# Gate stage stores transposed rows for the mixer, and the three stages run in one block

## The reference, cut to what matters

```python
xn  = layernorm(x)                              # no gain, no bias
# mixer
xin, xg = split(xn @ W_in.T)                    # 512 -> 2 x 1024
u   = silu(causal_conv4(xin) + conv_b)
Bu  = u @ W_B.T;  h_t = 0.95 h_(t-1) + 0.05 Bu_t    # 64 states, a scan over 2048 rows
y   = ((h @ W_C.T + D * u) * silu(xg)) @ W_out.T    # 1024 -> 512
a   = layernorm(y + xn) * g + b
# experts
gates = (tanh(xn @ gate_w.T) + 1) / 2           # 8 experts
idx   = top 1024 rows of each expert by its gate
o     = gelu(layernorm(xn[idx]) @ fc1.T + b1) @ fc2.T + b2      # 512 -> 2048 -> 512
out   = x + a + (xn with gates * o added at idx)
```

## Time and profile before

| what | value |
|---|---|
| median of 3 runs | 2914.63 us (2913.05 to 2925.31) |
| profiled execution, its own time | 2916.93 us |
| its span | 2915.2 us |
| mean granted TensorE clock | 0.986 |
| PE busy | 2794.6 us (96%) |
| DVE busy | 1849.0 us (63%) |
| ACT busy | 1309.0 us (45%) |
| POOL busy | 668.7 us (23%) |
| moved by DMA | 283.71 MB, mean 97 GB/s |

### The profile page before, as it was taken

One profiled execution on the slowest core, in us unless ns is written; L12 is line 12 of the kernel. 1 busy time (PEld: TensorE's weight loads), 2 busy tenths in 40 slices (PEclk: granted clock), 3 DMA queues, 4 the chain that ended last, 5 costly groups with the idle time before them and its releaser, 6 DMA issues.

```text
span 2915.2 us, 40359 instructions
## 1 busy us (share of the span) xinstructions
PE 2794.6 (96%) x12424; PEld 2234.5 (77%) x12426; DVE 1849.0 (63%) x3098; ACT 1309.0 (45%) x2197; POOL 668.7 (23%) x909
## 2 busy tenths in 40 slices
PE   7789999999999999999799999999999999999997
PEld 3367888888887778888687878888788787887886
DVE  6457777777777788888755554555545554455553
ACT  3354444443343355555344444444444444444443
POOL 2243222222222222223311221012210111102211
PEclk9899999999999999999899999999999999999999
DMA  7742333333333333336314133041330413304121
GB/s 270 255 139 92 108 111 109 111 112 115 115 115 116 116 88 108 96 105 210 106 34 119 30 94 81 18 128 30 94 80 16 123 37 87 77 26 123 38 44 15
DMA packets 130326, 283.71 MB, mean 97 GB/s; under 512 B 14640, under 2 KB 14832, under 8 KB 130032
## 3 DMA queue, kind: packets, MB, share of 16 engines
q1 hardware_dynamic: 98096, 183.71, 19.4%
q0 software_dynamic: 32064, 97.85, 13.8%
HBM read 226.68 MB, written 54.82 MB: 97 GB/s over the span
## 4 chain that ended last, share of the span: by engine, by line
PE 47%; issue 2%; DMA 1%; DVE 1%; POOL 0%; ACT 0%; DVEq 0%; POOLq 0%; SPq 0%
PE po L1661 8%; PE po L1662 8%; PE po L1663 8%; PE ph L1661 8%; PE ph L1663 7%; PE ph L1662 7%; PE f_pt L1670 1%; DMA out_dram<-res,idx_c 1%; DMA rows<-xn_rows,idx_c 0%; POOL out_dram L1530 0%; DMA b<-b_in 0%; DVE res L1643 0%; DVE f_stats L504 0%; DVE hid_l L1621 0%; DVE w2l L1587 0%
## 5 line engine op out<-in xcount | busy, mean ns | idle before, releaser
L1661 PE MATMUL po<-w2h,hid_h 128*128 128x512 f32 x1024 | 405.6, 396 | 14.3 <-DVE hid_l L1621 14.3
L1299 PE MATMUL ring<-xt_h,w_h 128*128 128x512 f32 x1024 | 402.5, 393 | 10.6 <-ACT sg L1029 9.2
L1662 PE MATMUL po<-w2l,hid_h 128*128 128x512 f32 x1024 | 403.1, 394 | 0.0
L1301 PE MATMUL ring<-xt_h,w_l 128*128 128x512 f32 x1024 | 402.0, 393 | 0.0
L1663 PE MATMUL po<-w2h,hid_l 128*128 128x512 f32 x1024 | 401.7, 392 | 0.0
L1300 PE MATMUL ring<-xt_l,w_h 128*128 128x512 f32 x1024 | 400.0, 391 | 0.0
L1621 DVE TENSOR_TENSOR hid_l<-xn_tail,hid_h 128x512 fp32r<-128x512 f32 x256 | 175.5, 685 | 331.8 <-ACT hid_h L1578 326.2
L1119 DVE SCALAR_TENSOR_TENSOR u<-xin,cw,u 128x512 f32<-128x512 f32 x384 | 295.4, 769 | 118.2 <-ACT u L1011 97.4
L1574 ACT ACTIVATE xn_tail<-ph,b1c 128x512 f32<-128x512 f32 x256 | 176.2, 688 | 357.1 <-PE ph L1663 348.9
L1530 POOL DMA_INDIRECT out_dram<-res,idx_c x64 | 109.4, 1709 | 898.8 <-DVE res L1643 884.2
L1548 ACT CAST w1h<-w1r 128x512 fp32r<-128x512 f32 x258 | 160.3, 621 | 280.1 <-PE po L1663 268.5
(11 more groups left out here) (176 smaller groups left out, 5561.9 us busy)
## 6 DMA issues: line engine op xcount, KB each, us to landing
wo<-wo_halves POOLq DMA_DIRECT2D x120, 512.0 KB, 4.1
w1r<-fc_in SPq DMA_DIRECT2D x130, 256.0 KB, 2.7
w2r<-fc_in SPq DMA_DIRECT2D x130, 256.0 KB, 2.9
xn_rows<-g_ext SPq DMA_DIRECT2D x16, 1040.0 KB, 5.3
w1r<-x_in SPq DMA_DIRECT2D x16, 1024.0 KB, 7.8
rows<-xn_rows SPq DMA_DIRECT2D x16, 1024.0 KB, 6.5
xn_tail<-xn_rows SPq DMA_DIRECT2D x64, 256.0 KB, 2.6
x_tail<-x_in SPq DMA_DIRECT2D x64, 256.0 KB, 2.9
```

Of the source, the lines that this page charges most:

```text
L1299: pe.matmul(ring[r % 2][:, :], w_h[:, r, q], xt_h[:, k, :], start=(k == 0), stop=False)
L1301: last = pe.matmul(ring[r % 2][:, :], w_l[:, r, q], xt_h[:, k, :], start=False, stop=(k == KD - 1))
L1661: pe.matmul(dst, ah, bh, start=start, stop=False)
L1662: pe.matmul(dst, ah, bl, start=False, stop=False)
```

## The change

- `xn_rows` is gone. The gate stage now stores the transposed rows, as ACT copied them out of the banks (1 MB for a block, `xt_rows`), and the gates alone (`gate_rows`, 8 numbers for a row). Normalising is in place and PE waits for all four tiles of a block.
- The mixer loads a turn's transposed rows as they are. Its 240 transposes are gone for turns 1 to 15; `xt_h` and `xt_l` are made from the loaded tile. The gate stage takes block 0 last, and makes turn 0's `xt_h` and `xt_l` from its own banks.
- The 16 tiles of the in-projection's weights are split in the gate stage, one for each block: ACT `w_high` behind the tanh, POOL `w_low` behind its work for the inverse deviation. POOL also gets four small instructions for each block that keep scale and shift of every row.
- The rows that the turns end with are made on ACT from `x`: `normal_rows` (for xn) and `sum_rows` (for x + xn, in place of POOL's `add_x`), four of each in a turn. The transfers into `xn_tail` are gone.
- The experts' rows are gathered from `x`, and the gates by a second gather (`gather_gates`), four more indirect transfers in a group; `keep` waits for them.
- One block holds all three stages, each engine goes from stage to stage by its own waits, and the semaphores are set once, by SP, behind the first two loads of `x`. Banks and tiles are laid over each other; the last block's gates are finished inside turn 0.

```diff
-        m.start()
-        with nc.Block() as block:
...
+    def turn(b, i):                       # POOL, gate stage
+            pool.tensor_scalar(std[:, :], mv[i % 2][:, :, 1], EPS, None, ALU.add).then_inc(c_eps, 1)
+            pool.wait_ge(c_eps, b + 1 + 1)
+            pool.tensor_tensor(rstd[i % 2][:, :], std[:, :], half[:, :], ALU.pow).then_inc(c_rs, 1)
+            pool.wait_ge(c_rs, b + 1 + 1)
+            pool.tensor_tensor(shift[i % 2][:, :], mv[i % 2][:, :, 0], rstd[i % 2][:, :],
+                               ALU.mult).then_inc(c_nb, 1)
...
+        def w_low(b, i):
+            tile = bass.ds(b, 1)
+            pool.wait_ge(c_wh, b + 1 + 1)
+            pool.sem_inc(p_tick, 1)
+            pool.tensor_tensor(w_l[:, tile, :].rearrange("p o d -> p (o d)"), w_raw[i][:, :],
...
+        with pool.Fori(1, NG - 1) as h:
+            for i in range(R):
+                turn(h * R + i, i)
+                w_low(h * R + i, i)
...
+        def group(h, first=False, last=False):          # ACT, gate stage
...
+                for k in range(KD):
+                    act.wait_ge(c_t, b * KD + k + 1 + 1)
+                    act.copy(xnt[i][:, k, :], pt[k][:, :]).then_inc(c_tc, 1)
+                    if last and i == R - 1:
+                        act.copy(ew.yt_h[0][:, k, :], pt[k][:, :]).then_inc(c_th, 1)
+                if not (first and i == 0):
+                    turn_tanh(act, b - 1)
+                if not (last and i == R - 1):
+                    w_high(b, h, i)
+                act.wait_ge(c_se, (b + 1) * KD + 1)
+                act.wait_ge(c_sc, b + 1)
+                act.copy(sc_t[:, :], pst).then_inc(c_sr, 1)
...
+    def normal_rows(self, act, b, j):
+        act.activation(self.xn_rows[j][:, :], self.x_rows[j][:, :], ACT.Identity, bias=self.row_shift[:, here],
+                       scale=self.row_scale[:, here]).then_inc(self.c_nr, 1)
...
+    def sum_rows(self, act, b, j):
+        act.activation(self.x_rows[j][:, :], self.x_rows[j][:, :], ACT.Identity, bias=self.row_shift[:, here],
+                       scale=self.twice[:, j:j + 1]).then_inc(self.c_s, 1)
...
             for k in range(KD):                        # ACT, end of a mixer turn
                 y_high(b, 4 + k)
                 side(4 + k)
-                if k >= lag:
-                    t_high((b + 1) * KD + k - lag, k - lag)
+                if not last:
+                    t_high(b, k)
+                elif k >= 1:
+                    group_high(k - 1)
+                ends.normal_rows(act, b, k)
...
-                        if 3 <= c < 7 and not last:
-                            next_turn(b, c - 3, False)
...
-            for j in range(J):                         # POOL, mixer turn
-                ends.add_x(pool, b - 1, j)
+            ends.twice_scale(pool, b - 1)
+            for j in range(J):
                 ends.add_beta(pool, b - 1, j)
...
+    def gather_gates(self, pool, g, j, i=0):
+        pool.wait_ge(self.c_mv, (g + 1) * J + 1)
+        pool.sem_inc(self.p_tick, 1)
+        pool.indirect_dma_start(
+            out=self.rows[:, j, D:XW], out_offset=None, in_=self.t["gate_rows"][:, :],
...
     def keep(self, dve, g, i):
+        for j in range(J):
+            dve.wait_ge(self.c_ga[j], 32 * (g + 1))
```

More of the change, by code:

```diff
@@ L45, in sb, with over @@
         return tile
[L47 to L69, removed]
+    def over(self, name, end, size, shape, dt=F32):
+        return self.nc.alloc_sbuf_tensor_at(name, shape, dt, offset=end - size)
 def f(ap):
@@ new lines, in stage_gate @@
+    tanh = m.sb("g_tanh", [P, J * E])
+    gw = m.sb("g_gw", [P, KD, E])
+    staged2 = m.over("g_staged2", ends.xn_end, J * D * 4, [P, 4, TB])
+    pt = banks[0:KD]
+    pst = banks[6][0:E, :]
+    psc = banks[7][:, 0:J * E]
+    w_raw = ends.res
+    w_h, w_l = ew.w1, ew.w2
+    c_id = m.count("g_id")
+    c_gw = m.count("g_gw_in")
+    c_x = [m.count(f"g_x_in{i}") for i in range(R)]
+    c_raw = ends.c_raw
+    c_wh = m.count("g_wh")
+    c_wl = sums.c_in_low
+    c_gd = sums.c_gate_rows
+    c_xs = sums.c_xt_store
@@ new lines, in turn_scores, with turn_tanh @@
+    def turn_scores(pe, b):
+        pe.wait_ge(c_sr, b + 1 + 1)
+        pe.wait_ge(c_ta, b + 1)
+        pe.sem_inc(t_tick, 1)
+        for j in range(J):
+            last = pe.transpose(psc[:, j * E:(j + 1) * E], sc_t[:, j * P:(j + 1) * P],
+                                ident[0:E, 0:E])
+        last.then_inc(c_sc, 1)
+    def turn_tanh(act, b):
+        act.wait_ge(c_sc, b + 1 + 1)
+        act.wait_ge(c_v, b * 2 + 1)
+        act.activation(tanh[:, :], psc, ACT.Tanh).then_inc(c_ta, 1)
@@ new lines, in stage_mixer @@
+    m = mem
+    w_h, w_l = ew.w1, ew.w2
+    xt_h, xt_l = ew.yt_h[0], ew.yt_l[0]
+    rows = ew.rows
+    w_raw = ends.res
+    ls = Lists(m, gates, thr, slots_d, ew, sums)
+    wo = m.sb("wo", [P, WO, 2, D], F32R)
+    u = m.sb("u", [P, NC_, TB])
+    u_h = [m.sb(f"u_h{i}", [P, TB], F32R) for i in range(2)]
+    u_l = [m.sb(f"u_l{i}", [P, TB], F32R) for i in range(2)]
+    y_h, y_l = u_h, u_l
+    sg = m.sb("sg", [P, SG, TB])
+    xin = [m.sb(f"xin{i}", [P, 3 + TB]) for i in range(2)]
+    halo = m.sb("halo", [P, NC_, 3])
@@ new lines, in stage_mixer @@
+    po, c_o, c_po = ends.po, ends.c_o, ends.c_po
+    p_tick, d_tick = ends.p_tick, ends.d_tick
+    c_win = ends.c_raw
+    c_wo = [m.tick(f"m_wo{s}") for s in range(WO)]
+    c_ws = m.count("m_ws")
+    c_rows = m.count("m_rows")
+    c_set = m.count("m_set")
+    c_wh = m.count("m_wh")
+    c_wl = m.count("m_wl")
+    c_ag = m.count("m_ag")
+    c_x = m.count("m_x")
+    c_hi = m.count("m_hi")
+    c_ho = sums.c_ho
+    c_ev = m.count("m_ev")
+    c_cv = sums.c_cv
+    c_u = m.count("m_u")
+    c_uh = m.count("m_uh")
@@ L873, in _ @@
-                with sp.Fori(1, LAST) as b:
-                    turn(b)
-                for dst, src in ((ew.gamma, t["f_ln_g"]), (ew.beta, t["f_ln_b"])):
-                    sp.dma_start(dst[:, :], src.to_broadcast([P, D])).then_inc(ew.c_small, 16)
-                last_turn(LAST)
+                gate[0](sp)
+                mixer[0](sp)
+                experts[0](sp)
             @block.gpsimd
             def _(pool):
-                pool.memset(ends.half[:, :], -0.5).then_inc(c_set, 1)
@@ L1709, in build @@
[L1709 to L1726 removed]
+                gate[4](act)
@@ L1729 @@
+                mixer[4](act)
+                experts[4](act)
 SHAPES = {
```

2327 lines of the change are left out of this document (1199 added, 1128 removed).

## The result

The changed kernel takes 2905.84 us, the median of 6 runs (of which one took 7964.04 us and is left out of the comparison; the others lie between 2903.56 and 2908.58), against 2916.68 us for the kernel before in 6 runs. The ratio is 0.9958, with a 95% interval of 0.9945 to 0.9972. The profiled execution has a span of 2906.9 us against 2915.2, so 8.3 us less.

What follows compares the result with a forecast made beforehand. PE is busiest; some 70 us of its idle time lie before turn 1 and at turn 15. Terms 18.8 - 20.4 + 3 - 5 - 4.8 = -8.4 against 2916.93 give 2908.5, as a median 2906 us; range 2880 to 2936.

Steps and rivals of the forecast that it cites:

- Gate stage: Gate stage: loop ACT, POOL, DVE, PE gives 9.3 us a block (8.37 to 9.77); turn 0 starts 18.8 us later.
- Turn 0: Mixer's first turn: without step-by-step weight feed 77.0 us instead of 97.39, bounds 74.5 and 80; -20.4 us.
- Turns 1 to 14: Mixer: DVE sets the pace, so removed transposes give -2 us; normal_rows lengthens hot turns by 5; together +3 us.
- Turn 15: Last mixer turn: POOL's additions no longer overlap DVE's normalising; -5 us, bounds 0 and -8.
- Into the experts: Expert entry: PE's 7.09 us wait falls to some 2.8 without a barrier; with b2's earlier load -4.8 us.
- In the experts: Expert groups: second gather delays keep by 2.4 us, hidden from PE with about 1 us to spare; 0 us.
- the clock that holds: Rival, gate stage: clock holds or falls seldom; -14 us, 2892 us; chance 0.16.
- The shorter loop: Rival, gate stage: loop absent or shorter, blocks at DMA's 6.9 us; -36 us, 2870 us; chance 0.04.
- The gained transposes: Rival, mixer: PE gains the time of its removed transposes; -22 us, 2884 us; chance 0.05.
- The longer loop: Rival, gate stage: POOL's instructions clash with DVE's normalising, 1.9 us more a block; +28 us, 2934 us; chance 0.09.
- ACT's rows in every turn: Rival, mixer: ACT's rows cost 1.65 us in ten more turns; +17 us, 2923 us; chance 0.07.
- The late second gather: Rival, experts: gates' gather lands late, each of 16 groups loses 2 us; +32 us, 2938 us; chance 0.07.

Runs made afterwards that it cites:

- experiment 1: Changed kernel with POOL's inverse deviation of the next block ahead of w_low in the gate stage: 2873.4 us, 0.9857 of the kernel before.
- experiment 3: Changed kernel with 16 transposes of a constant tile put back on PE in each of turns 0 to 14: 2910.1 us.
- experiment 4: Changed kernel with all four normal_rows behind the last y_high in turns 0 to 14: 2898.55 us; hot turns together 319.7 against 326.0.
- experiment 5: Kernel before with POOL's eight additions for turn 15 moved to the start of the expert stage: 2924.94 us.
- experiment 6: Kernel before with experts' rows gathered from x, gates left out: 2916.5 us; then both kernels unedited again: before 2912.05, changed 2906.7 us.
- experiment 2: Changed kernel with extra PE work behind gate blocks' scores: five score matmuls 2919.69 us, two 2908.9, 16 constant-tile transposes 2897.94.

## Why the prediction was right

It said 2906 us and no change that can be told from the noise, nearly faster; measured are 2905.84 us, 0.4% less. The 95% interval (0.9945 to 0.9972) excludes no change, so these runs tell the two kernels apart more finely than the half per cent that the prediction took as its limit. Most steps were right in mechanism. That the total is so close is luck: the errors of the terms, up to 5 us each, cancel.

| term | forecast | measured |
|---|---|---|
| start of turn 0 | +18.8 | 162.17 - 142.95 = +19.2 |
| turn 0 | -20.4 | 79.67 - 97.39 = -17.7 |
| turns 1 to 10 | -2 | 768.85 - 772.44 = -3.6 |
| hot turns | +5 | 326.01 - 320.15 = +5.9 |
| turn 15, to its last transposes | -5 | 80.14 - 86.70 = -6.6 |
| from there to the second layer's first product | -4.8 | 14.2 - 16.7 = -2.5 |
| from there to the last matmul | 0 | 1456.1 - 1461.2 = -5.1 |
| from there to the end | 0 | 19.70 - 17.66 = +2.0 |
| sum | -8.4 | -8.3 |

**Gate stage.** The loop was there as walked, link by link, at both clocks (8.31 and 9.81 us against 8.37 and 9.77), and experiment 1 shows that it sets the step. The clock held in 4 of 15 steps; I had taken one in three. The first transposes came at 14.3 and not 15.9, but the first step took 11.3 us. That evened out.

**Turn 0.** The mechanism held (the step-by-step feed of weight tiles is gone, with it the wait of 9.24 us), the size was 2.7 us off. PE waited for `u_l` before its matmul at 227.12, for 1.49 us, and the clock fell there:

```profile
224.00:230.00 6.00, 4.24 (x13) 0.76 0.25 98
```

(a stretch of PE alone, as in the earlier trace rows). ACT and POOL split the out-projection's tiles beside that chain; whether this makes it late wasn't tried.

**Turns 1 to 14.** DVE's unbroken chain swallowed the transposes' gain (experiment 3), and one `normal_rows` costs 0.53 us three times in a hot turn (experiment 4), as said.

**Turn 15.** The clash of POOL with DVE was the cause (experiment 5); its price was 6.3 us and not 5.

**Into the experts.** The first wait fell by 4.3 us as forecast, but the term ended there. What ACT does next was not followed: rows of turn 15, then a wait for DVE. This step of the prediction, "some 2.8 us" and a gain of 4.8, was half given back two steps later.

**In the experts.** `keep` waits for the second gather, 41.0 us over 16 groups or 2.56 each (the forecast was 2.4, though its own numbers, 3 x 1.26 + 3.8 - 5, give 2.6), and PE feels none of it, as said. But "groups unchanged" came out only in the sum, from two changes that the prediction lacked. PE from the second layer's first product to the last matmul, in two executions of the kernel before, then in two of the changed one:

```profile
1436.32:2897.54 1461.22, 1444.38 (x6376) 1.00 0.26 65
1435.89:2892.71 1456.82, 1440.48 (x6376) 1.00 0.26 65
...
1431.03:2887.15 1456.12, 1450.44 (x6375) 1.00 0.26 65
1428.73:2885.77 1457.04, 1449.98 (x6375) 1.00 0.26 65
```

PE's idle time (length less busy time) fell from 16.3 to 16.8 us to 5.7 to 7.1, by the waits of experiment 6. Its busy time grew by 6 to 10 us for the same matmuls: 12 of them take 2.79 us in the mean where nothing interrupts them, against 2.77, which over 512 such steps is some 9 us (an estimate). So the -5.1 us of the table is no stable gain: the second execution of the kernel before is as short here as the changed kernel. Both causes stay open. Missed too were the 2.0 us at the end of the program: all profiles of the changed family have 19.2 to 19.7 us behind the start of the last matmul, against 17.4 to 17.7. The issue of the last scatter ends 9.4 us behind that matmul in both kernels, so the difference lies behind it; no run here explains it.

Of the rivals, the clock that holds is refuted by the trace of the changed kernel (0.87 in the stage) and priced by experiment 2. The shorter loop is refuted by the step of 9.35 us. The gained transposes fall by experiment 3. The longer loop falls by the steps, and by DVE's normalising, which takes 1.91 us beside POOL as it did before; ACT's rows in every turn fall by the turns themselves. The late second gather falls by PE's waits.

## What to carry to other kernels

Before an instruction is added to an engine's queue, write down what it waits for and who waits for what stands behind it. Here one subtraction of 1.3 us, placed ahead of an instruction that was ready long before, closed a loop through four engines and cost 35 us of the gate stage; a change of order gave it back (32 us of the whole kernel). Work taken off an engine is worth only what that engine is late by: 15 us of transposes gave 3.7. And follow a removed wait to the next place where the same chain is due, since a gain that is counted at the first matmul can be gone at the tenth.

## What the runs showed of the hardware

- A DVE instruction of 0.69 us took 10.23 us while POOL ran eight additions back to back (experiment 5). I had priced such a clash at 1 us, from one instruction. Here it lasted as long as POOL's unbroken run, but not every DVE instruction waits for the whole run: in the changed kernel the copy of b1 at 1421.11 took 1.27 us instead of 0.17 and ended at 1422.38, as the first of POOL's four additions (1420.93 to 1422.34) did, while the others ran on to 1426.1. What decides between the two was not tried.
- Float32 transposes kept the granted clock at 1.00 as well as matmuls did, as 2 us of either filled an idle time of 2.4 us (experiment 2).
- In the expert stage a step of 12 matmuls takes 2.72 us in one of two neighbouring groups of the kernel before and 2.76 to 2.82 in the other (medians of a group). In the changed kernel all groups have 2.75 to 2.81. The granted clock is 1.00 in both, the shapes are the same, and the cause was not tried further.
